# First batch, weights' place and the end of batch 30 in a graph layer of 32 batches on one core

## The reference

```python
u = jnp.einsum('bld,bmd->blm', h, h) / jnp.sqrt(jnp.asarray(d, h.dtype))
p = jax.nn.softmax(u, axis=-1)
delta = p * adjacency
attn = delta / (jnp.sum(delta, axis=2, keepdims=True) + 1e-10)
h_left = jnp.einsum('bld,ed->ble', h, W_left) + b_left      # h_self, h_right likewise
attn_left = jnp.where(j > i, attn, 0.0)
attn_right = jnp.where(j < i, attn, 0.0)
ctx = einsum(attn_left, h_left) + diag_a[..., None] * h_self + einsum(attn_right, h_right)
o = (ctx - mu) / jnp.sqrt(var + LN_EPS) * gamma + beta      # over the 384 features
return _layernorm(x + jax.nn.relu(o), axis=-1)
```

## Time and profile before

| what | value |
| --- | --- |
| three executions | 460.93, 461.45, 461.82 us, median 461.45 |
| the profiled execution's own time | 460.66 us |
| its span | 458.9 us (458.93) |
| PE busy | 449.3 us, 98% |
| DVE, ACT, POOL busy | 387.9 (85%), 322.5 (70%), 208.7 (45%) |
| mean granted clock of PE | 0.996 |

### The profile page before, as it was taken

How to read it: one execution, slowest core, us unless ns; L and a number is a source line. 1 busy time by engine, 2 the same in 40 slices (tenths; PEclk the granted TensorE clock), 3 DMA queues, 4 the chain that set the end, 5 groups by cost and what they waited for, 6 DMA issues and landing times.

```text
span 458.9 us, 9720 instructions
## 1 busy us (share of the span) xinstructions
PE 449.3 (98%) x2639; PEld 446.9 (97%) x2639; DVE 387.9 (85%) x1366; ACT 322.5 (70%) x710; POOL 208.7 (45%) x293
## 2 busy tenths in 40 slices
PE   8999999999999999999999999999999999999993
PEld 7999999999999999999999999999999999999992
DVE  5877988888898888988788888788988888988786
ACT  5756677767678767677667678677677677677753
POOL 0144346543345553445643345653345553345642
PEclk9999999999999999999999999999999999999998
DMA  7765455665455665455556546566555666454222
GB/s 246 237 206 180 129 174 181 199 196 188 127 194 194 189 194 185 148 180 190 187 194 189 157 165 195 186 194 196 151 173 181 190 203 188 152 171 157 91 68 94
DMA packets 84135, 80.60 MB, mean 176 GB/s; under 512 B 7058, under 2 KB 76436, under 8 KB 84116
## 3 DMA queue, kind: packets, MB, share of 16 engines
q1 hardware_dynamic: 84112, 80.38, 54.8%
q10 hardware_dynamic: 4, 0.00, 0.0%
HBM read 52.04 MB, written 28.31 MB: 175 GB/s over the span
## 4 chain that ended last, share of the span: by engine, by line
PE 91%; DVE 2%; DMA 2%; POOL 1%; ACT 1%; SPq 1%; issue 1%; POOLq 0%; DVEq 0%; ACTq 0%
PE ps_proj L482 61%; PE ps_ctx L526 20%; PE ps_scores L474 3%; PE ps_scores L470 2%; PE ps_scores L468 2%; PE ps_scores L420 1%; DMA w_raw<-in_L_gnn_W_left 1%; SPq L319 1%; DMA dt_dram<-turned 1%; DMA dt_raw<-dt_dram 0%; PE ps_proj L504 0%; DVE stats L841 0%; POOL rstd L1099 0%; ACT normed L634 0%; SPq L342 0%
## 5 line engine op out<-in xcount | busy, mean ns | idle before, releaser
L482 PE MATMUL ps_proj<-w_hi,xt_split 128*128 128x384 f32 x1152 | 304.0, 335 | 0.1
L482 PEld LDWEIGHTS ps_proj<-w_hi,xt_split 128*128 128x128 f32 x1152 | 209.1, 188 | 0.7 <-ACT ps_proj L604 0.5
L482 PE MATMUL ps_proj<-w_lo,xt_split 128*128 128x384 f32 x576 | 192.7, 334 | 0.0
L1099 POOL TENSOR_TENSOR rstd<-var_eps,minus_half 128x4 f32<-128x4 f32 x31 | 34.9, 1127 | 186.2 <-DVE var_eps L856 186.2
L482 PEld LDWEIGHTS ps_proj<-w_lo,xt_split 128*128 128x128 f32 x576 | 108.1, 188 | 0.0
L604 ACT ACTIVATE ps_proj<-bias 128x384 f32<-128x384 f32 x188 | 90.3, 494 | 1.0 <-DVE proj_lo L826 0.9
L1105 POOL TENSOR_TENSOR scaled<-normed,gamma_sb 128x384 f32<-128x384 f32 x60 | 61.6, 1027 | 30.4 <-ACT normed L634 30.4
L608 ACT ACTIVATE proj_hi<-ps_proj 128x384 fp32r<-128x384 f32 x128 | 63.4, 496 | 16.4 <-PE ps_proj L482 16.1
L628 ACT ACTIVATE ps_ctx<-ps_proj,diag 128x384 f32<-128x384 f32 x64 | 35.5, 555 | 53.4 <-PE ps_proj L482 53.4
L826 DVE TENSOR_TENSOR proj_lo<-ps_proj,proj_hi 128x384 fp32r<-128x384 f32 x128 | 67.3, 544 | 2.0 <-ACT proj_hi L608 1.9
L1109 POOL TENSOR_TENSOR shifted<-scaled,beta_sb 128x384 f32<-128x384 f32 x61 | 62.3, 1021 | 2.5
(11 more groups left out here) (100 smaller groups left out, 656.9 us busy)
## 6 DMA issues: line engine op xcount, KB each, us to landing
x_sb<-in_x SPq DMA_DIRECT2D x32, 384.0 KB, 4.4
xt_sb<-in_x_t SPq DMA_DIRECT2D x31, 384.0 KB, 3.8
out_dram<-out_sb SPq DMA_DIRECT2D x31, 384.0 KB, 2.9
adj_sb<-in_adj SPq DMA_DIRECT2D x32, 256.0 KB, 4.4
dt_dram<-turned SPq DMA_DIRECT2D x31, 256.0 KB, 2.0
dt_raw<-dt_dram SPq DMA_DIRECT2D x124, 64.0 KB, 2.0
cross_dram<-cross_turned SPq DMA_DIRECT2D x29, 256.0 KB, 2.0
cross_raw<-cross_dram SPq DMA_DIRECT2D x116, 64.0 KB, 2.0
```

The costliest lines, as they stand in the source:

```text
L482: mm = nc.tensor.matmul(ps_proj[bank(at, g)][:, 0:H], stationary, moving[w][:, c, :], start=(clear and i == 0), stop=True, skip_group_chec ...
```

## The change

Five things change together.

1. The warm-up is seven matmuls on the constant 0.0 that the program has from its start, and waits for nothing. The open matmul behind them still waits for `zeros`.
2. The rows have 33 partitions, partitions 0 and 32 each holding both biases, the rest zero (DVE sets them first). ACT rounds all 33, DVE subtracts on partition 32 only, so that partition 0 holds the rounded and 32 the rest, and `two_ones`, with ones on 0 and 32, adds both in one matmul for each tile. The four rows are loaded on POOL's queue after DVE's memset.
3. RIGHT's weight is loaded in three chunks, each with its semaphore. ACT and DVE split the rows between LEFT's second and third chunk, and DVE's `finish_scores` comes after RIGHT's first.
4. In the last batch DVE does all three steps of near's tile 1; near's residual statistics move behind final's, into buffers of their own; near's output on ACT, power on POOL and store on SP come after final's tile 0.
5. `weights_place` (32 bytes per partition) moves weights, bias, gamma, beta, x, xt and adj from 32 to 64 modulo 128 bytes in a partition; `xt_place` (96 bytes) leaves all behind it at its residue.

The diff, cut to its core:

```diff
+        sb("weights_place", [P, 8])
         w_raw = [sb(f"w_raw{w}", [P, C, H]) for w in range(3)]
...
+        sb("xt_place", [P, 24])
...
+        rows = sb("rows", [LO + 1, 2, H])
+        rows_split = sb("rows_split", [LO + 1, 2, H], F32R)
+        two_ones = sb("two_ones", [LO + 1, P], F32R)
...
-            load_weight(RIGHT)
+            for w in (LEFT, RIGHT):
+                for c in range(C):
+                    sp.dma_start(w_raw[w][:, c, :], w_rows[w][:, c, :]).then_inc(chunk_loaded[w, c], 16)
...
-                for t in range(T):
-                    for row in (rows_hi, rows_lo):
-                        mm = nc.tensor.matmul(ps_proj[bank(at, GROUPS.index((w, t)))][:, 0:H], ones_row[:], row[:, w, :], start=False,
+                for t in range(T):
+                    nc.tensor.matmul(ps_proj[bank(at, GROUPS.index((w, t)))][:, 0:H], two_ones[:], rows_split[:, w, :], start=False,
+                                     stop=True, skip_group_check=True).then_inc(proj_ready, 1)
...
+            none = nc.const_aps.tensor(0.0, (P, H), F32).bitcast(F32R)
+            for i in range(WARM_UP):
+                nc.tensor.matmul(ps_proj[i % PBANKS][:, 0:H], none[:, 0:P], none, start=True, stop=True)
             pe.wait_ge(zeros_ready, 1)
-            for i in range(WARM_UP):
-                open_bank(ps_proj[i % PBANKS][:, 0:H])
...
+                act.wait_ge(rows_loaded, 4 * 16)
+                nc.scalar.activation(rows_split[:], rows[:], ACT.Copy).then_inc(rows_hi_ready, 1)
...
+            nc.vector.memset(rows[:], 0.0).then_inc(rows_zeroed, 1)
...
+            pool.wait_ge(rows_zeroed, 1)
+            for w, vector in ((LEFT, b_left), (RIGHT, b_right)):
+                for row in (0, LO):
+                    nc.gpsimd.dma_start(rows[row:row + 1, w, :], vector.partition_broadcast(1)).then_inc(rows_loaded, 16)
...
-                    act.wait_ge(shift_ready, before.n(1, 1))
-                    nc.scalar.activation(normed[:, 1, :], ps_ctx[:, 1, 0:H], ACT.Identity, bias=shift[before.slot(2)][:, 1:2],
-                                         scale=rstd[before.slot(2)][:, 1:2]).then_inc(near_normed_ready, 1)
...
+                near_add(before, 0)
+                centre(1, near_scaled_ready)
+                near_add(before, 1)
                 split_proj(at, 2)
...
+            store_tile(0)
+            sp.wait_ge(out_ready, near.n(T, T + 1))
+            sp.dma_start(out_rows[BATCHES - 2], out_sb[near.slot(2)][:]).then_inc(stored[near.slot(2)], 16)
```

More of the change, by code:

```diff
@@ L84, in gnn_resnorm @@
     BY_PE = 4
-    WARM_UP = 6
+    WARM_UP = 7
+    LO = 32
     LARGEST = 3.0e38
@@ L195, in gnn_resnorm @@
         first_xt_loaded = [sem(f"first_xt_loaded{c}") for c in range(C - 1)] + [xt_loaded[0]]
-        left_loaded = [sem(f"left_loaded{c}") for c in range(C)]
-        w_loaded = {RIGHT: sem("right_loaded"), SELF: sem("self_loaded")}
+        chunk_loaded = {(w, c): sem(f"{name}_loaded{c}") for w, name in ((LEFT, "left"), (RIGHT, "right")) for c in range(C)}
+        self_loaded = sem("self_loaded")
         rows_loaded = sem("rows_loaded")
         bias_loaded = [sem(f"bias_loaded{w}") for w in range(3)]
-        ones_row_ready = sem("ones_row_ready")
+        two_ones_ready = sem("two_ones_ready")
+        rows_zeroed = sem("rows_zeroed")
         rows_hi_ready = sem("rows_hi_ready")
@@ L648, in _ @@
             first = Batch(0, 0)
-            for w, vector in ((LEFT, b_left), (RIGHT, b_right)):
-                act.dma_start(rows[:, w, :], vector.partition_broadcast(1)).then_inc(rows_loaded, 16)
             split_first_xt()
-            for c in range(C):
-                split_weight(LEFT, c)
+            split_weight(LEFT, 0)
+            split_weight(LEFT, 1)
             split_rows()
+            split_weight(LEFT, 2)
             for c in range(C):
@@ L736, in _ @@
             end = Batch(BATCHES // UNROLL, 0)
-            outputs(end.plus(-2))
             final = end.plus(-1)
@@ L743, in _ @@
             nc.scalar.activation(to[:, 0, :], y[:, 0, :], ACT.Identity, bias=sh[:, T:T + 1], scale=rs[:, T:T + 1]).then_inc(out_ready, 1)
+            outputs(end.plus(-2))
             act.wait_ge(last_centred_ready, 1)
@@ L883, in split_rows @@
                 dve.wait_ge(rows_hi_ready, 1)
-                nc.vector.tensor_tensor(rows_lo[:], rows[:], rows_hi[:].bitcast(F32), ALU.subtract).then_inc(rows_lo_ready, 1)
+                row = slice(LO, LO + 1)
+                nc.vector.tensor_tensor(rows_split[row], rows[row], rows_split[row].bitcast(F32), ALU.subtract).then_inc(rows_lo_ready, 1)
             def split_weight(w, c):
@@ L900, in _ @@
                                         ).then_inc(xt_lo_ready, 1)
-            for c in range(C):
-                split_weight(LEFT, c)
+            split_weight(LEFT, 0)
+            split_weight(LEFT, 1)
+            split_rows()
+            split_weight(LEFT, 2)
+            split_weight(RIGHT, 0)
             finish_scores(first)
-            split_rows()
-            for c in range(C):
-                split_weight(RIGHT, c)
+            split_weight(RIGHT, 1)
+            split_weight(RIGHT, 2)
             dve.wait_ge(moments_ready, 1)
@@ L1037, in _ @@
             dve.wait_ge(vectors_loaded, 2 * 16)
-            dve.wait_ge(near_shifted_ready, 1)
+            dve.wait_ge(near_shifted_ready, T)
             centre(0, last_scaled_ready)
[L1041 to L1046, removed]
             dve.wait_ge(x_loaded[final.slot(UNROLL)], final.loads(UNROLL, 1))
@@ L1051, in _ @@
             last_add(0)
-            dve.wait_ge(near_rstd_ready, 1)
-            nc.vector.scalar_tensor_tensor(shift[own][:, T:2 * T], moments[:, T:2 * T, 0], -1.0, rstd[own][:, T:2 * T],
-                                           ALU.mult, ALU.mult).then_inc(shift_ready, 1)
             residual_stats(final, 0)
+            near_residual_stats(0)
             split_proj(final, 3)
@@ L1067, in _ @@
             last_add(1)
+            dve.wait_ge(near_rstd_ready, 1)
+            nc.vector.scalar_tensor_tensor(shift[own][:, T:2 * T], near_moments[:, :, 0], -1.0, rstd[own][:, T:2 * T],
+                                           ALU.mult, ALU.mult).then_inc(shift_ready, 1)
             residual_stats(final, 1)
```

92 lines of the change are left out of this document (46 added, 46 removed).

## The result

The changed kernel took 469.94 us in the median of six runs (466.79 to 470.18) against 461.29 us before: ratio 1.0179, 95% interval 1.0161 to 1.0197. It is 8.65 us slower; 460.8 was forecast, range 459.6 to 462.4. The profiled execution is the fastest of the six, 466.79 us of its own time with a span of 465.0 and a mean granted clock of PE of 0.996; the other five took 469.9 to 470.2 us at 0.986 to 0.989. So there are two losses: one in every run, some 6.1 us against the profiled run of before, and one of about 3 us more in five of six, which comes with a lower clock.

What follows compares the result with a forecast made beforehand. PE's matmul stream was taken to bound the kernel between start and tail. Median: 461.45 - 0.87 (bias) + 0.45 (tail) - 0.2 (warm-up) = 460.8 us, with placement at 0; range 459.6 to 462.4.

Steps and rivals of the forecast that it cites:

- signs of being wrong: Listed in advance: rounding after 6.5, RIGHT's first product after 11.06, batches not 13.75, last store's distance change outside 0.2 to 0.9.
- Placement: All batches: moving weights from 32 to 64 modulo 128 bytes taken as 0; up to 1.2 us hidden, gain or loss.
- rival B: Start: rows land after 6.5, stalling ScalarE, VectorE and PE; 460.8 + (T-6.5), 462.8 at T = 8.5; chance 0.22.
- T: Start: when the bias rows land; taken as 6.1, in time, bounds 4.8 and 8.5; 7.05 from the skill page.
- T minus 6.5: First batch: PE's stall in us if the rows land at T, later than 6.5.
- Bias, if the rows are in time: First batch: RIGHT's first product at 10.54 instead of 11.06 (0.52), two fewer matmuls in RIGHT's block (0.35); gain 0.87.
- Warm-up: Start: warm-up matmuls on a constant begin about 0.5 earlier; median gain 0 to 0.5, taken as 0.2.
- Tail: Last batches: final context stats 0.23 later, near's store just ahead of the last one; cost +0.45, at most 0.9.
- nothing is late there: Tail: near's three VectorE operations fit an idle of 1.2 us before split_proj 2 and one stats' place; no delay.
- rival E: Whole kernel: 32-byte shift costs PE or VectorE up to 1.2, or the 33-row matmul is slow; 461.2 to 462.1; chance 0.08.

Runs made afterwards that it cites:

- e1: Kernel before with only the placement changed (weights, bias, x, xt, adj at 64 instead of 32 modulo 128 bytes): 465.67 us against 461.17, ratio 1.0088.
- e5: The changed kernel with both placement buffers taken out, weights back at 32 modulo 128 bytes: 463.76 us against 461.19, ratio 1.0042.
- e6: e3 with the four row loads issued by ScalarE's queue behind one small activation, instead of by POOL: 460.26 us against 461.19, ratio 0.9982.
- e3: Kernel before with only the first batch's change (33-row bias matmul, rows loaded by POOL, RIGHT's weight in three loads, split order): 464.17 us against 461.17.
- e9: e3 with ten matmuls of zeros into free banks while PE waits for LEFT's third chunk: 462.20 us against 460.96, ratio 1.0025.
- e2: Kernel before with only the seven warm-up matmuls on the constant zero: 461.30 us against 461.17, ratio 0.9998.
- e11: e6 with the seven warm-up matmuls on the constant: 460.22 us against 460.96, ratio 0.9981.
- e4: Kernel before with only the tail's change (batch 30's norm on VectorE, its statistics, output and store later): 461.78 us against 461.17, ratio 1.0011.
- e12: e11 with the change's tail too (whole change, old weight placement, rows loaded by ScalarE's queue): 460.94 us against 460.96, ratio 0.9997.

## Why the prediction was wrong

The forecast was 460.8 and the result 469.94. Two terms of the sum failed: the placement, put at 0, and the start, where the rows came late and the lower clock was not counted. Three of the prediction's own signs of being wrong came true: ACT's rounding of the rows starts at 8.12, after 6.5; RIGHT's first product at 12.38, later than 11.06; steady batches take 13.89, not 13.75.

- **Placement: "So I take 0", and 1.2 us as the most it could cost.** It costs 4.5 us (e1), and 6.1 on top of the rest (e5). The bound was taken from products that all had the same distance between their two tiles, and from one matmul of zeros, whose stationary and moving operand are the same tile. Those rows could say nothing on another distance, and the change alters it: the weights move by 32 bytes, xt_split by 128. The row showed the steady state of one placement, and the text took it for a bound on all.
- **Rows late, rival B at 0.22.** Late rows are what happened; T was 8.10, not 6.1. The terms that failed are the start and the flight, not the issue. POOL's first issue started at 2.81, 0.65 behind the memset (predicted at once). The four issues took 2.17, 0.54 each (0.52 taken), and ended at 4.98. The last row landed 3.1 us behind that, where the flight of a store, 1.9, was taken. By the prediction's own formula T = 8.10 gives a stall of 1.6; PE went on at 10.60, 1.74 behind the 8.86 of before, and with the bias gains the start cost 0.98. The figures of the Trainium skill, page "DMA: Bandwidth & Descriptors" (Specifications, and the fixed cost in Anatomy of one DMA), led the prediction to T = 7.05, nearer than the rows did. That sum counted three issues where the one from rows counts four; with four it comes to 8.05, near the 8.10 by chance, as an issue took 0.54 and not 1. The Trainium skill says on the same page, Issuing engine by pattern, that the path of sync and scalar is generally faster. That is borne out: e6 differs from e3 by the queue and one small activation, and is 3.9 us faster, of which some 1.8 is the clock's.
- **The price of being late, "T minus 6.5".** Half was missing. With PE's pause the mean granted clock is lower in eight of eleven runs of e3 and in five of six of the change. This costs 1.8 us in the median of e3 (against e9, where the pause is filled) and 3.1 in those five; the trace of e5 shows the 1.2 GHz level for over 6 us behind the pause. The prediction spoke of the clock only for the warm-up. The Trainium skill, page "TensorE: Matmul & The Clock Gate", Part 1, says that the throttled state is the default and activity releases it. The trace of e5 agrees: 0.50 behind a pause of 2.34 us, and 1.00 again from about 17.5, with PE at work.
- **Bias, if the rows are in time: gain 0.87.** This was right: e6 is 0.93 faster, with RIGHT's first product at 10.44. The change of shape cost 0.27 with 33 rows too (the last product starts at 9.62, the bias matmul at 9.89).
- **Warm-up: 0 to 0.5, take 0.2.** It gave nothing (e2, e11).
- **Tail: +0.45.** It was +0.6 to +0.7 (e4, e12 against e11). The mechanism was right, near's statistics ahead of the final ones and near's store ahead of the last: the final stats came at 451.91 for 451.69, the last operation at 456.56 for 456.42. The step "nothing is late there" was off by 0.1: split 2 came at 445.15 for 445.04, behind near's three operations, PE's last matmul of tile 0's context ended 0.1 later, and its stats started at 446.24 for 446.13. The hand-over from POOL's rstd to the scaling took 0.2 where 0.05 was counted (448.04 for 447.80).

Both sides of slower were there: rival B with 0.22, priced without the clock, and rival E with 0.08, which named the shift by 32 bytes and priced it at 1.2 at most. The largest term of all stood at 0.

## What to carry to other kernels

Before moving a tile, work out what the move does to its distance from the tiles it is used with, modulo 256 bytes, and not only to its own residue; time the placement by itself, since one row of the same placement cannot bound it. When a load moves behind a new wait or to another queue, count the wait's hand-over, each issue and the flight from a row of that queue, and if there is none, treat the time from issue to landing as unknown, up to the 4 us seen here. Price a pause of PE of about 2 us as the pause and what the clock may lose after it; where the pause can't go, matmuls of zeros into a free bank were cheap cover here (e9).

## What the runs showed of the hardware

- A stream of matmuls with 384 moving columns starts 173.3 ns apart at distances of 0, 32, 64 and 224 bytes modulo 256 between stationary and moving tiles (7.80 us for 45, up to 7.82 at 32), but 176.7 ns at 96 and 176.0 at 128 (7.95 and 7.92). What makes it so is not known; distances of 160 and 192 were not run.
- PE's clock fell behind a single pause of 2.34 us in full stream (e5) and did not behind one of 1.70 (the change) or 1.22 (e3) in other runs; with the same program the mean clock is low in some runs and not in others (e3: 0.987 to 0.994).
- Loads of 1.5 KB issued by POOL landed 3.0 to 3.6 us behind the start of their issue in the change, and 2.7 to 4.2 us in e3, while the weights were loading.
